# A scan layer and a routed expert layer on one core: the first two slots of 256 rows as one unit of 512, and the loads and turns that go with it

## The reference

```python
x = x + attn(layernorm(x))        # attn: h = rmsnorm(x) * gamma; q, kv, a = split(h @ w_qkva.T)
                                  # y[n] = sigmoid(a[n]) * y[n-1] + kv[n]; result q * y
x = x + ffn(layernorm(x))
# ffn: logits = z @ router_w.T; top 2 of 7 experts, weights softmax(top values)
#      expert: h = silu(z @ w_gate) * (z @ w_up); h @ w_down     (hidden 1024)
#      mixed = sum of the two experts' rows by weight + one shared expert for every row
```

## Time and profile before

| | us |
|---|---|
| median of 3 runs | 985.65 (985.25 to 985.87) |
| profiled execution | 986.29 |
| its span | 984.5 |
| PE busy | 973.7 (99%) |
| PE weight loads busy | 849.3 (86%) |
| DVE busy | 587.9 (60%) |
| ACT busy | 477.5 (49%) |
| POOL busy | 396.8 (40%) |

### The profile page before, as it was taken

One profiled execution on the slowest core, in us unless ns is written; L12 is line 12 of the kernel. 1 busy time (PEld: TensorE's weight loads), 2 busy tenths in 40 slices (PEclk: granted clock), 3 DMA queues, 4 the chain that ended last, 5 costly groups with the idle time before them and its releaser, 6 DMA issues.

```text
span 984.5 us, 15882 instructions
## 1 busy us (share of the span) xinstructions
PE 973.7 (99%) x5565; PEld 849.3 (86%) x5565; DVE 587.9 (60%) x1042; ACT 477.5 (49%) x769; POOL 396.8 (40%) x265
## 2 busy tenths in 40 slices
PE   8999999999999999999999999999999999999997
PEld 6888998888889998888888888888888999999886
DVE  7988687788663134455445544654465455656576
ACT  4565434322422325446545554554455566667563
POOL 3336100000021243464645463655465588776200
PEclk9999999999999999999999999999999999999999
DMA  9433300000059995634463456355634576774393
GB/s 324 115 87 86 87 22 22 17 6 22 1 142 353 317 305 177 198 125 147 163 204 111 150 176 197 88 174 175 202 88 167 187 264 231 271 213 160 120 298 107
DMA packets 146018, 155.06 MB, mean 157 GB/s; under 512 B 75433, under 2 KB 134322, under 8 KB 138802
## 3 DMA queue, kind: packets, MB, share of 16 engines
q1 hardware_dynamic: 139232, 136.08, 42.7%
q0 software_dynamic: 6720, 18.36, 5.9%
q10 hardware_dynamic: 18, 0.01, 0.0%
HBM read 127.67 MB, written 26.74 MB: 157 GB/s over the span
## 4 chain that ended last, share of the span: by engine, by line
PE 88%; DVE 5%; DMA 2%; ACT 2%; issue 1%; SPq 1%; POOL 0%; DVEq 0%; ACTq 0%; POOLq 0%
PE ps L1150 38%; PE ps L1128 15%; PE ps L1106 11%; PE ps L1131 8%; PE ps L1012 6%; PE ps L1172 4%; PE ps L1192 3%; DMA sorted_rows<-x_stage 2%; PE ps L994 1%; PE ps L1200 1%; SPq L447 1%; ACT h_hi L878 1%; PE ps L1023 1%; DVE h_lo L1748 1%; DVE ps L1742 1%
## 5 line engine op out<-in xcount | busy, mean ns | idle before, releaser
L1150 PE MATMUL ps<-xs_hi,w_both 128*128 128x512 f32 x1216 | 380.4, 391 | 0.1
L1150 PEld LDWEIGHTS ps<-xs_hi,w_both 128*128 128x128 f32 x1216 | 228.3, 188 | 49.1 <-DVE ps L1742 1.2
L644 POOL TENSOR_TENSOR w_both<-w_raw,w_both 128x2048 fp32r<-128x2048 f32 x45 | 223.5, 4967 | 106.2 <-ACT w_both L815 97.6
L1150 PE MATMUL ps<-xs_lo,w_both 128*128 128x512 f32 x608 | 236.7, 389 | 0.0
L1128 PE MATMUL ps<-w_both,h_hi 128*128 128x512 f32 x656 | 233.0, 398 | 0.1
L1131 PE MATMUL ps<-w_both,h_lo 128*128 128x256 f32 x656 | 184.1, 281 | 0.0
L1748 DVE TENSOR_TENSOR h_lo<-ps,h_hi 128x512 fp32r<-128x512 f32 x152 | 105.2, 692 | 103.6 <-ACT h_hi L878 82.2
L668 POOL DMA_INDIRECT x_stage<-z_rows,idx_x x70 | 73.4, 1048 | 224.5 <-DVE idx_x L1661 160.9
L1742 DVE TENSOR_TENSOR ps<-ps,silu 128x512 f32<-128x512 f32 x152 | 106.3, 699 | 91.9 <-ACT silu L871 63.3
L871 ACT ACTIVATE silu<-ps 128x512 f32<-128x512 f32 x152 | 90.8, 597 | 134.0 <-PE ps L1150 133.8
L1128 PEld LDWEIGHTS ps<-w_both,h_hi 128*128 128x128 f32 x656 | 123.3, 188 | 30.2 <-DVE h_lo L1748 0.4
(11 more groups left out here) (228 smaller groups left out, 1080.8 us busy)
## 6 DMA issues: line engine op xcount, KB each, us to landing
w_raw<-in_L_ffn_w_gate_dram SPq DMA_DIRECT2D x20, 1024.0 KB, 4.9
w_raw<-in_L_ffn_w_up_dram SPq DMA_DIRECT2D x20, 1024.0 KB, 7.3
w_raw<-in_L_ffn_w_down_dram SPq DMA_DIRECT2D x20, 1024.0 KB, 6.1
sorted_rows<-x_stage SPq DMA_DIRECT2D x32, 256.0 KB, 2.2
x_rows<-sorted_rows SPq DMA_DIRECT2D x128, 64.0 KB, 2.0
w_spare<-in_L_ffn_w_up_dram SPq DMA_DIRECT2D x6, 1024.0 KB, 6.6
w_spare<-in_L_ffn_w_gate_dram SPq DMA_DIRECT2D x6, 1024.0 KB, 10.0
w_spare<-in_L_ffn_w_down_dram SPq DMA_DIRECT2D x6, 1024.0 KB, 12.9
```

The source lines that it names most:

```text
L644: pool.tensor_tensor(w_lo[buf][:, k, :], w_raw[buf][:, k, :], w_hi[buf][:, k, :].bitcast(F32), ALU.subtract).then_inc(wlo_ready[k], 1)
L1150: last = pe.matmul(ps[:, 2 * (j % 2) + part, :], w[:, part, kd * H + j * P:kd * H + (j + 1) * P], xx[:, h // 2, kd, :], start=i == 0, stop ...
```

## The change

The two slots 0 and 1 become one `quad(0, 0, ...)` on PE, ACT and DVE. Unit 0 is turned two groups earlier (group 5), and unit 1 in group 7 where unit 0 was (`UNIT_AT`), each with its x_lo between the halves of that group's scan, and its x_hi on ACT after the sigmoid of that group, ahead of `h_rows(g + 2)`. `turn_back(g)` for these groups waits for x_split too. The work that stood in the slots is spread over the new unit: on PE the last turning back first of all, the routings before j = 2, 4 and 7, the last z transpose before j = 5, into banks 4 and 5, waiting for the residual of the last group in place of gated; the rank matmuls after the first tile of the narrow half. On DVE the totals, blocks and quarters of the ranking stand between the two additions after the down projection, the kinds behind the unit, the places in the next one. Units 2 and 3 are loaded ahead of the store of the last group's z, and turned in the new unit.

```diff
+        UNIT_AT = {NC - 3: 0, NC - 1: 1}
@@ SP
+            for n in (2, 3):
+                load_x(n, n, z_dram, n % 2)
             store_z(NC - 1)
             sp.wait_ge(z_out[NC - 1], 16)
-            for n in range(2, SA):
+            for n in range(4, SA):
                 load_x(n, n, z_dram, n % 2)
@@ ACT
-                act.activation(zT[NC - 1][:, :, :], ps[:, 0:2, :], ACT.Copy).then_inc(zT_ready, 1)
+                act.activation(zT[NC - 1][:, :, :], ps[:, 4:6, :], ACT.Copy).then_inc(zT_ready, 1)
...
-                elif g < NC - 2:
-                    h_rows(g + 2)
+                else:
+                    if g in UNIT_AT:
+                        x_hi(UNIT_AT[g], UNIT_AT[g])
+                    if g < NC - 2:
+                        h_rows(g + 2)
                 if g + 1 < NC:
                     h_hi_part(g + 1)
-                else:
-                    x_hi(0, 0)
...
-            slot(0, 0, early=True, turns=((2, 1),), between={1: lambda: z_rows(NC - 1), 2: zT_copy})
-            slot(1, 1, early=True, turns=((1, 1), (3, 2)))
+            quad(0, 0, early=True, between={1: lambda: z_rows(NC - 1), 5: zT_copy})
@@ PE
             def turn_last_z():
                 pe.wait_ge(z_ready, NC)
-                pe.wait_ge(gated, 5)
+                pe.wait_ge(res_ready, NC)
...
+                if g in UNIT_AT:
+                    pe.wait_ge(x_split, UNIT_AT[g] + 1)
...
+                    if t == ST and JH + 1 in between:
+                        between[JH + 1]()
...
-            slot(0, 0, 0, between={0: last_back, 2: lambda: last_routes(NC - 3),
-                                   6: lambda: last_routes(NC - 2), JH - 1: turn_last_z},
-                 down=lambda: last_routes(NC - 1), skip=0)
-            slot(1, 1, 0, between={1: ranks}, skip=0)
+            quad(0, 0, 0, skip=0, wide=False, between={
+                0: last_back, 2: lambda: last_routes(NC - 3), 4: lambda: last_routes(NC - 2), 5: turn_last_z,
+                7: lambda: last_routes(NC - 1), JH + 1: ranks})
@@ DVE
-                if g == NC - 1:
-                    turn_x(0, LD)
-                scan(g, None if g + 1 < NC else lambda: x_lo(1, 0))
+                if g in UNIT_AT:
+                    n = UNIT_AT[g]
+                    turn_x(n, LD)
+                    scan(g, lambda: x_lo(n + 1, n))
+                else:
+                    scan(g)
...
-            slot(0, 0, turns=((1, 1, loads(1)),), shared=0, early=True, skip=0, between={
-                ("gated", 0): lambda: statistics2(NC - 1), 1: logits_and_z,
-                2: lambda: take_logits(NC - 2, 7), "down": choices})
-            slot(1, 1, turns=((0, 1, loads(2)), (2, 2, loads(3))), shared=1, early=True, skip=0, between={
-                0: rank_totals, 1: rank_blocks, 2: rank_quarters, "down": kinds_and_places})
+            quad(0, 0, turns=ahead_of(0), shared=0, early=True, skip=0, between={
+                ("gated", 0): lambda: statistics2(NC - 1), 2: logits_and_z, 5: lambda: take_logits(NC - 2, 7),
+                "down": choices, "half": totals_and_blocks})
+            rank_kinds()
             betweens = {
-                2: {0: pair_targets, 3: lone_places, 6: lone_targets, 7: find_pairs, "down": move_all,
+                2: {0: places, 2: pair_targets, 3: lone_places, 6: lone_targets, 7: find_pairs,
+                    "down": move_all,
```

More of the change, by code:

```diff
@@ L984, in turn_last_z @@
                         z = z_all[:, (NC - 1) * CT + k, :].rearrange("p (i k) -> p k i", k=KD)
-                        last = pe.transpose(ps[:, kd, k * P:(k + 1) * P], z[:, kd], ident[:, :])
+                        last = pe.transpose(ps[:, 4 + kd, k * P:(k + 1) * P], z[:, kd], ident[:, :])
                 last.then_inc(zT_psum, 1)
@@ L1792, in quad @@
                     gate(n, j, par, early, skip, ps[:, 2 * par + 1, :].rearrange("p (j n) -> p j n", j=2))
+                    if ("gated", j) in between:
+                        between["gated", j]()
                     rest(n, j, par, early, skip, h_lo[:, j, :].rearrange("p (j n) -> p j n", j=2),
@@ L1845, in logits_and_z @@
                 turn_z(NC - 2)
-            def kinds_and_places():
-                rank_kinds()
-                places()
             def move_all():
@@ L1865, in lists, with totals_and_blocks @@
                 hot_cols(c)
-            slot(0, 0, turns=((1, 1, loads(1)),), shared=0, early=True, skip=0, between={
-                ("gated", 0): lambda: statistics2(NC - 1), 1: logits_and_z,
-                2: lambda: take_logits(NC - 2, 7), "down": choices})
-            slot(1, 1, turns=((0, 1, loads(2)), (2, 2, loads(3))), shared=1, early=True, skip=0, between={
-                0: rank_totals, 1: rank_blocks, 2: rank_quarters, "down": kinds_and_places})
+            def totals_and_blocks():
+                rank_totals()
+                rank_blocks()
+                rank_quarters()
             def ahead_of(n):
                 return ((1, 2, loads(n + 2)), (4, 3, loads(n + 3)))
+            quad(0, 0, turns=ahead_of(0), shared=0, early=True, skip=0, between={
+                ("gated", 0): lambda: statistics2(NC - 1), 2: logits_and_z, 5: lambda: take_logits(NC - 2, 7),
+                "down": choices, "half": totals_and_blocks})
+            rank_kinds()
             betweens = {
-                2: {0: pair_targets, 3: lone_places, 6: lone_targets, 7: find_pairs, "down": move_all,
+                2: {0: places, 2: pair_targets, 3: lone_places, 6: lone_targets, 7: find_pairs,
+                    "down": move_all,
                     "half": lambda: first_places(0)},
```

## The result

The changed kernel takes 995.55 us (median of 4, 994.96 to 996.12) against 985.62; the ratio is 1.0098, with a 95% interval of 1.0086 to 1.011. The profiled execution lasted 996.12 us with a span of 994.4. 4.2 us more were forecast; it is 9.9. The four executions lie in two pairs, 996.12 and 996.09, 995.01 and 994.96, and the profiled one is of the longer pair.

The account below looks back on a forecast made before the run. PE, busy 99% at full clock, bounds the kernel. Terms -1.83 + 1.91 + 1.9 + 0.95 + 0.15 + 0.5 + 0.7 give +4.3, taken as 4.2: median 985.65 to 989.8 us, range 987.0 to 992.3.

Parts of the forecast that it names:

- Work on PE: Slots to new unit: gate/up gains 1.27 us, down loses 0.16, old waits of 0.72 go; net 1.83 us gained.
- wait 4: After the first narrow down tile, PE waits 0.15 us for the choices before the rank matmuls; bounds 0 and 0.6.
- 1, turning back: At the hand-over, PE waits 1.91 us for DVE's scan and product with q before the last group's transposes.
- 2, routing of group 6: Before j = 4 of the new unit, PE waits 1.9 us for DVE's z transpose; bounds 1.5 and 2.5.
- 3, routing of group 7: Before j = 7 of the new unit, PE waits 0.95 us for ACT's zT copy; bounds 0.5 and 1.5.
- 5, group 6: In the scan stage, x_lo between the scans and x_hi delay PE's start of group 6 by 0.5 us; bounds 0, 0.9.
- 6, unit 2: In the next unit, moved places and pair_targets make PE wait 0.7 us for gate(3) at j = 5; bounds 0, 1.5.
- rival (c): PE's clock falls in the new waits; two stretches of a j at half clock give 995 us; chance 0.05.
- (a): Only the hand-over wait is real, the others hidden: 985.7 us, no change; chance 0.1, with half-way cases up to 987.6.
- (b): The longer moving operand pays off and all waits vanish, hand-over included: 983.8 us or a little less; chance 0.06.
- (d): DVE's backlog after the ranking holds gate(0) of unit 2; wait 6 becomes 1.5 to 3: 990.6 to 992.2; chance 0.14.
- Queues passed: SP's eight more loads ahead of the last store are free, ending at 110.4 while the store waits until 113.04.

Follow-up runs that it names:

- e5: The changed kernel with last turning back, last z transpose and its copy, group 6's z transpose and logits moved to other table entries: 985.98 us (0.9999).
- e9: The changed kernel with 9, 10 and 5 extra matmuls, their results overwritten, inside the three waits of the new unit: 991.56 us (1.0054).
- e3: The changed kernel with the logits of group 5 and z transpose of group 6 on VectorE behind rest(1) instead of rest(2): 990.95 us (1.0052).
- e4: The changed kernel with the last z transpose on TensorE before j = 4 and its ScalarE copy behind the rounding of j = 4: 994.71 us (1.0094).
- e1: The changed kernel with 8, 8 and 4 extra matmuls, their results overwritten, inside the three waits of the new unit: 992.76 us (1.0064).
- e6: The kernel before, slots kept, with only the last turning back put ahead of the first matmul of slot 0: 988.82 us (1.0029).

## Why the prediction was wrong, step by step

**Work on PE: right.** The unit without waits lasts 41.63 us in e5 for 43.23 with its old waits of 0.72, 1.6 gained for 1.83 forecast; 0.14 of the difference is wait 4, which e5 has.

**The waits: right in place, in releaser and in order, somewhat small in size.**

| wait | forecast | measured |
|---|---|---|
| 1, turning back | 1.91 | 2.20 |
| 2, routing of group 6 | 1.9 | 2.31 |
| 3, routing of group 7 | 0.95 | 1.12 |
| 4, rank matmuls | 0.15 | none (0.14 in e5 and e9) |
| 5, group 6 | 0.5 | 0.44 |
| 6, unit 2 | 0.7 | 0.80 |

Waits 1 to 3 are longer in good part because PE's first start behind a wait comes 0.26 to 0.36 us after its releaser, not 0.06 as in the earlier trace rows. The forecast took that distance from a short wait. Of the 0.29, 0.41 and 0.17 us by which the three exceed their terms, this makes 0.3, 0.2 and 0.2. DVE and ACT rows of the changed kernel:

```profile
101.14 1.22 DVE L1359 TENSOR_TENSOR y_sb<-ps,y_sb 128x1024 f32<-128x1024 f32 x1
...
118.76 1.29 DVE L1329 STREAM_TRANSPOSE zT<-z_in 128x512 f32<-128x512 f32 x2
...
132.75 1.01 ACT L782 ACTIVATE zT<-ps 128x1024 f32<-128x1024 f32 x1
```

The product ends at 102.36 and PE starts at 102.72; the transpose at 120.05, PE 120.31; the copy at 133.76, PE 134.02. Wait 4 did not come: the half clock reached into the first down matmuls and made PE 0.2 us later there, just the size of that wait. With the clock full it is there: in e5 the rank matmuls start at 138.13 and were due at 137.99.

**The sum: wrong by the clock.** The step that failed is the term for the clock: the sum has none, and the case that it falls was left to rival (c). That rival had the right mechanism and the right time, 995, but a chance of 0.05, and the range stopped at 992.3. The reasoning was that no row showed a fall for a wait of about 1.9 us. But no row showed a wait of that length at full clock either: the longest of the rows was 0.48 us (the whole trace has one of 0.73, at 10.94 us), and the 0.55 at the end was a row that spoke for the fall. Absence of a case was read as evidence against it. The filled kernel puts the price at about 4.7 us over three stretches, 1.6 each, where (c) had two of 2.7, a whole j each; that its 995 is so near to 995.55 is in part luck. The rule of the Trainium skill that was cited (TensorE: Matmul & The Clock Gate, Part 1) is borne out by the windows here: idleness in the three waits, half clock behind them, full clock when the waits are filled. It is borne out as a direction only, since waits of 1.12 us (e3) and 2.20 us (e4) also passed at full clock.

With the clock full and the rest as it came, the kernel takes 991.56 (e9). The sum, 989.8, is 1.8 short of that: 0.7 are waits 1 to 3 (5.45 in e9 for 4.76), 0.1 is the wait in unit 2, and the remainder was not taken apart. The prediction's own terms also give 46.2 for the stretch to unit 2, and not the 46.1 that it names.

**Rivals (a), (b) and (d).** (a) fell: waits 3 and 5, under 1.2 us, are as real as the long ones. (b) describes what the change could have been, 985.98 in e5. (d) fell: gate(0) of unit 2 was not held up; the wait there is 0.80, and the stretch is 1.0 longer.

**Queues passed: right.** The eight loads ahead of the store cost nothing that e5, which keeps them, would show.

## What to carry to other kernels

Where the engine that sets the time is full, a wait is worth more than its length: here each wait of 1.1 to 2.3 us cost some 1.6 us more through the clock whenever a fall followed it, so price both, and give the clock a real chance whenever a change makes a wait longer than any that the trace shows. When work is moved from a fine-grained loop to a coarse one, ask for each entry whether it now stands before or behind the first block of matmuls and which engine's step it needs; five table entries decided between 985.98 and 995.55 us. And before believing in a long stretch of small losses, fill the waits with matmuls whose results are dropped: that separates the clock from the schedule in one or two kernels. Look at more than one execution too: here a single profile could show a fall or miss it.

## What the runs showed of the hardware

- The clock can fall well after PE has resumed, and in none of the waits traced here was it seen at half: full from 120 to 122, with the wait ended at 120.31, and half from 124 to 126. Behind the hand-over it fell with the first matmuls (0.74 from 102 to 104, PE back at 102.72). PE shows as busy throughout; only starts (0.43 for 0.227 us) and the granted clock tell.
- No single length of a wait decides. A wait of 2.20 us at the hand-over was followed by a fall in the changed kernel and not in the profile of e4, with the same instructions up to there; one of 1.12 us was in the changed kernel and not in the profile of e3; a rest of 0.34 us, with sixteen matmuls of 7 columns behind it, was in the profile of e1; 0.48 us in the kernel before was not, nor were 0.44 and 0.80 in the changed one. What exactly decides was not settled.
- The same kernel falls into steps of time (e1: 992.8 or 990.9; e6: five of six at 988.7 or more, one at 987.26), which the clock would explain. Only one execution of each kernel was traced, and the kernel before, too, has single executions up to 987.6, so the share of runs with a fall is not shown.
- In e4, with eight short transposes and sixteen routing matmuls right behind a wait, the slow stretch was twice as long (half clock in all three windows from 120 to 126). That they prolong it is a guess from this one profile.
- After the waits of 1 us and more PE started 0.25 to 0.36 us after its releaser ended (e6: 101.82 to 102.07); after those of 0.44, 0.48 and 0.80 us it was 0.05 or 0.06.
